# Attention of an iteration a quarter of its places later, where the second expert stream runs alone, and without the filler transposes

## What is computed

```python
x = x + 0.5 * _L0_ffn_ref(_layernorm(x), router_w, w1, w2)      # stream f1
x = x + _L0_attn_ref(_layernorm(x), W_qkv, W_out)               # stream at
x = x + 0.5 * _L0_ffn_ref(_layernorm(x), router_w, w1, w2)      # stream f2

# experts: 8 of them, widths 4 x 128 and 4 x 256; each token takes the best two
probs = sigmoid(xf @ router_w.T); topw, sel = top_k(probs, 2); topw /= topw.sum() + 1e-20
y = sum over the chosen e of topw_e * (relu(xf @ W1[e]) ** 2) @ W2[e]

# attention: 16 heads of 8, no softmax
q_feat = elu(rope(q) * SCALE) + 1;  k_feat = elu(rope(k)) + 1
kv = einsum('bhtd,bhtv->bhdv', k_feat, v);  k_sum = k_feat.sum(axis=2)
out = einsum('bhtd,bhdv->bhtv', q_feat, kv) / max(einsum('bhtd,bhd->bht', q_feat, k_sum), 1e-6)
x = x + out.reshape(B, T, D) @ W_out
```

## Time and profile before

| | us |
|---|---|
| median of 3 runs | 780.99 (779.64 to 781.48) |
| the profiled execution, its own time | 781.09 |
| its span, first to last instruction | 779.3 |
| mean granted TensorE clock | 0.991 of full |

### The profile page before, as it was taken

The page is one execution under the profiler, slowest core; times in us unless marked ns, Lnnn a source line. Parts: engine busy times, 40 slices in busy tenths (PEclk is TensorE's granted clock), DMA queues, the critical chain, the costliest instruction groups (busy, mean ns, idle before and its releaser), DMA issues.

```text
span 779.3 us, 13297 instructions
## 1 busy us (share of the span) xinstructions
PE 728.0 (93%) x3736; PEld 595.7 (76%) x3736; DVE 583.5 (75%) x1832; ACT 597.2 (77%) x1220; POOL 686.9 (88%) x664
## 2 busy tenths in 40 slices
PE   6799898789999999999999999999999998989887
PEld 6676676678888888888888888888887877767765
DVE  4767887877778786978788787978686777676543
ACT  4688768577888888798888888797879675766765
POOL 3899887769999999999999999999999868666886
PEclk9999999999999999999999999999999999999999
DMA  5553312312233333312233333313123303303330
GB/s 183 190 191 109 109 24 87 109 47 79 95 110 123 109 124 109 120 64 87 87 108 123 109 124 110 120 45 127 66 109 122 124 2 108 123 1 123 122 123 27
DMA packets 31160, 79.38 MB, mean 102 GB/s; under 512 B 3312, under 2 KB 14448, under 8 KB 31088
## 3 DMA queue, kind: packets, MB, share of 16 engines
q1 hardware_dynamic: 30800, 78.47, 29.7%
q10 hardware_dynamic: 288, 0.07, 0.1%
HBM read 73.81 MB, written 4.72 MB: 101 GB/s over the span
## 4 chain that ended last, share of the span: by engine, by line
POOL 26%; PE 26%; DVE 23%; issue 11%; ACT 8%; DMA 3%; DVEq 1%; POOLq 0%; ACTq 0%; SPq 0%
POOL h_lo L906 16%; DVE hid L1093 6%; POOL root_f L900 4%; PE bank L517 3%; PE bank L519 3%; PE bank L537 3%; PE bank L518 3%; PE bank L539 3%; PE bank L538 3%; ACT h_hi L763 2%; DMA g_all_f<-rows_f 2%; POOL x_lo_at L894 2%; DVE pick_f L1071 2%; PE bank L498 2%; PE bank L613 2%
## 5 line engine op out<-in xcount | busy, mean ns | idle before, releaser
L906 POOL TENSOR_TENSOR h_lo<-hid,h_hi 128x512 fp32r<-128x512 f32 x384 | 494.0, 1313 | 59.0 <-ACT h_hi L763 58.6
L1093 DVE SCALAR_TENSOR_TENSOR hid<-bank,g_all_f 128x512 f32<-128x512 f32 x384 | 263.3, 686 | 133.0 <-PE bank L519 93.9
L752 ACT ACTIVATE hid<-hid 128x512 f32<-128x512 f32 x384 | 229.2, 624 | 40.1 <-DVE hid L1093 40.0
L763 ACT ACTIVATE h_hi<-hid 128x512 fp32r<-128x512 f32 x384 | 226.4, 623 | 4.9 <-ACT hid L752 0.8
L517 PE MATMUL bank<-x_hi_f,w_hi 128*128 128x512 f32 x384 | 164.3, 428 | 13.7 <-DVE hid L1093 13.5
L537 PE MATMUL bank<-h_hi,w_hi 128*128 128x512 f32 x384 | 154.4, 402 | 7.1 <-POOL h_lo L906 6.9
L539 PE MATMUL bank<-h_hi,w_lo 128*128 128x512 f32 x384 | 152.6, 397 | 0.0
L519 PE MATMUL bank<-x_hi_f,w_lo 128*128 128x512 f32 x384 | 152.4, 397 | 0.0
L518 PE MATMUL bank<-x_lo_f,w_hi 128*128 128x512 f32 x384 | 152.1, 396 | 0.0
L538 PE MATMUL bank<-h_lo,w_hi 128*128 128x512 f32 x384 | 151.9, 396 | 0.0
L517 PEld LDWEIGHTS bank<-x_hi_f,w_hi 128*128 128x128 f32 x384 | 73.2, 191 | 37.0 <-DVE hid L1093 21.5
(11 more groups left out here) (112 smaller groups left out, 1053.7 us busy)
## 6 DMA issues: line engine op xcount, KB each, us to landing
g_all_f<-rows_f SPq DMA_DIRECT2D x128, 512.0 KB, 5.5
x_sb<-in_x SPq DMA_DIRECT2D x16, 256.0 KB, 3.0
out_x<-x_sb SPq DMA_DIRECT2D x16, 256.0 KB, 7.1
g_all_f<-in_w SPq DMA_DIRECT2D x2, 768.0 KB, 6.5
con<-in_const SPq DMA_DIRECT2D x1, 584.0 KB, 6.0
rows_f<-g_row_f SPq DMA_DIRECT2D x32, 16.0 KB, 1.4
g_all_f<-in_wqkv SPq DMA_DIRECT2D x1, 192.0 KB, 6.4
con<-in_const ACTq DMA_DIRECT2D x1, 68.0 KB, 3.0
```

The source lines that it names most:

```text
L752: fn(h, h, ACT.Square).then_inc(s_sq[s], 1)
L763: fn(h_hi[:, c, :], hid[:, c % STAGE, :], ACT.Copy).then_inc(s_hhi[s], 1)
L906: gp.tensor_tensor(h_lo[:, c, :], hid[:, c % STAGE, :], h_hi[:, c, :].bitcast(F32), ALU.subtract).then_inc(s_hlo[s], 1)
L1093: v.scalar_tensor_tensor(hid[:, c % STAGE, :], hp[c % 2][:], 0.0, g_all[s][:, EXPERT[c], :], ALU.max, ALU.mult).then_inc(s_z[s], 1)
```

## The change

In the iterations where f2 runs alone (t = 15, 16, 17) every part of attention from state to projection stands later: on TensorE state, attend, attn_transpose and out_proj each by a quarter (three jobs), on VectorE the mask by a place and the three steps of normalisation together behind weighted(10), on ScalarE the copy of the transposed attention behind the squares of quarter 4. add_attention stays where it was. The 16 filler transposes ahead of state are gone, 48 in all. Other iterations are not touched.

```diff
             def state(n):
                 pe.wait_ge(A["v"], value(n * BG + BG))
-                if alone("f2", n + 1):
-                    keep_busy(a1, 16)
                 pe.wait_ge(A["kf"], value(n + 1))
...
     TensorE, iteration(t, par)
                 quarter(t, 0, par)
-                state(t - 2)
+                if not alone("f2", t - 1):
+                    state(t - 2)
                 logits("f1", t + 2)
...
                 quarter(t, 1, par)
+                if alone("f2", t - 1):
+                    state(t - 2)
                 weight_rows("f2", t + 1 - SHIFT, t, 1)
-                attend(t - 2)
+                if not alone("f2", t - 1):
+                    attend(t - 2)
                 quarter(t, 2, par)
+                if alone("f2", t - 1):
+                    attend(t - 2)
                 transpose("at", t - 1, t, 2)
                 quarter(t, 3, par)
-                attn_transpose(t - 2)
+                if not alone("f2", t - 1):
+                    attn_transpose(t - 2)
...
                 quarter(t, 4, par)
-                out_proj(t - 2)
+                if alone("f2", t - 1):
+                    attn_transpose(t - 2)
+                else:
+                    out_proj(t - 2)
                 q(t - 1)
                 logits("f2", t + 2 - SHIFT)
                 quarter(t, 5, par)
+                if alone("f2", t - 1):
+                    out_proj(t - 2)
...
     ScalarE, iteration(t, par)
                 squares(t, 3)
-                copy_attnT(t - 2)
+                if not alone("f2", t - 1):
+                    copy_attnT(t - 2)
                 evacuate_x("f2", t + 2 - SHIFT, t, 2)
...
                 exp_logits("f2", t + 2 - SHIFT)
                 squares(t, 4)
+                if alone("f2", t - 1):
+                    copy_attnT(t - 2)
                 squares(t, 5)
...
     VectorE, iteration(t, par)
-                mask_state(t - 2)
+                if not alone("f2", t - 1):
+                    mask_state(t - 2)
                 weighted(t, 5)
                 best_two("f1", n1)
+                if alone("f2", t - 1):
+                    mask_state(t - 2)
                 weighted(t, 6)
...
                 weighted(t, 10)
+                if alone("f2", t - 1):
+                    normalise(t - 2, 0)
+                    normalise(t - 2, 1)
+                    normalise(t - 2, 2)
                 high_part("at", t - 1, 0)
```

More of the change, by code:

```diff
@@ L1227, in iteration @@
                 weighted(t, 7)
-                normalise(t - 2, 0)
+                if not alone("f2", t - 1):
+                    normalise(t - 2, 0)
                 weigh_two("f1", n1, 0)
                 weighted(t, 8)
-                normalise(t - 2, 1)
+                if not alone("f2", t - 1):
+                    normalise(t - 2, 1)
                 weigh_two("f1", n1, 1)
                 weighted(t, 9)
-                normalise(t - 2, 2)
+                if not alone("f2", t - 1):
+                    normalise(t - 2, 2)
                 weighted(t, 10)
+                if alone("f2", t - 1):
+                    normalise(t - 2, 0)
+                    normalise(t - 2, 1)
+                    normalise(t - 2, 2)
                 high_part("at", t - 1, 0)
```

## The result

The changed kernel takes 783.85 us (median of 16 runs, 782.02 to 787.4), the kernel before 780.17 us (778.25 to 782.32, 16 runs): ratio 1.0048, 95% interval 1.0036 to 1.006. That is 3.7 us slower. The forecast was 785.4, range 781.5 to 787.5, slower.

What follows compares the result with a forecast made beforehand. No engine is full in t = 15 to 17, so order and waits set the length, through VectorE's add_attention. Waits for the copy +2.3 and clock falls +2.1 give +4.4 us on 780.99: 785.4, range 781.5 to 787.5.

Steps and rivals of the forecast that it cites:

- order part: From q_features to add_attention: waits for the copied attention cost +0.3, +1.1, +0.9 us in t = 15, 16, 17, sum +2.3.
- clock part: In t = 15 to 17: clock falls behind new TensorE idle cost 3.15 us if all three occur; 2.1 taken.
- Fillers cost nothing on the path and cover the clock: Ahead of state: the 16 transposes lie beside TensorE's 1.35 us wait; removal saves 0 us, but they cover the clock.
- The mask is not later: VectorE's mask in t = 16: at about 668.05 against 668.20 before, though state is 1.9 us later.
- its wait on weighted(0): TensorE in t = 16: up(4) needs the bank weighted(0) empties at 664.70 to 665.38; a mask over 1 us later contradicts this.
- The logits' gain: Router logits in t = 16: done at 678.9, so exp at 678.95 against 680.10, a gain of 1.15 us.
- The projection waits for ScalarE's copy: TensorE's projection, t = 15 to 17: waits 1.4 to 1.8 us for the transposed attention's copy, now behind squares and copies.
- VectorE's unbroken half behind it passes all of this on.: From add_attention to the next q_features: VectorE works without a pause, so the whole +2.3 us delay passes on.
- Two falls of three were taken: Three new idle gaps of 3.1 us: two clock falls assumed, 2.1 us, each low stretch some 3.4 us.
- a fall begins only behind its wait: TensorE's clock: a fall starts after the idle wait ends (724, wait ended 723.20), a reason to take two of three.
- With the clock held: Rival 1: the clock holds through the new idle, only the copied-attention waits remain, +2.3 us, 783.3; chance 0.27.
- rival 2: ScalarE's copy is in time and projection goes right behind down(17): t = 15 to 17 sum -1.3 us, 779.8; chance 0.12.

## Why the prediction was right, and where it was not

- **Sign and size.** +3.7 us measured, +4.4 forecast, from an order part (2.3) and a clock part (2.1). The runs give 0.9 and 2.8. One part was too large by 1.4 and the other too small by 0.7, so that the total came within 0.7 us is partly luck.
- **Fillers cost nothing on the path and cover the clock.** Right: taking them out alone cost 2.7 us, and from q to a the loss lies in the two iterations in which the clock fell.
- **The mask is not later.** Right where the clock holds: with the fillers back it starts 3.93 us behind q_features in t = 16, forecast 3.95, before 4.10. In the changed kernel it starts 6.01 us behind, over 1 us later, which the prediction took for a sign that its wait on weighted(0) is wrong. It was not that, but the low clock. The iterations of the changed kernel, 33.8 and 30.5 us, also lie outside the forecast 31 to 33.
- **The logits' gain.** Direction right, size not: with the fillers back, exp starts 15.30 us behind q_features against 16.00 before, a gain of 0.70 in place of 1.15. The step that was off is x_hi_at behind the three steps of normalisation: 11.54 us behind q_features against 10.57 before, 1.0 later and not 0.5: weighted(10), which stands ahead of them, ended 10.05 us behind q_features and not 9.6.
- **The projection waits for ScalarE's copy.** Right in each iteration, 1.13 to 1.15 us where I had 1.4 to 1.8. What follows from it, q to a with the fillers back: forecast +0.3, +1.1, +0.9; measured -0.03, +1.59, +1.10, with the caveat above on the first.
- **"VectorE's unbroken half behind it passes all of this on."** This is the step that failed. It read "works without a pause" as "fixed in length". (The half that the prediction gives as 683.63 to 664.10 runs from 653.39 to 664.10, and the next from 683.63 to 694.32.) In that half cw_f was 0.5 us too long in t = 15 and 16, and 1.0 in t = 17, held by GpSimd; a later add_attention finds GpSimd's operation over and gets this back. With the 0.8 of the tail, the order part was therefore 0.9, not 2.3.
- **The clock.** The idle was right (3.1 forecast; 3.10, 3.24, 3.22). Two falls of three were taken, three came in the profiled execution, and the one in t = 16 lasted 7 us, not 3.4. Against the run with fillers back the falls cost 1.27, 2.47 and 0.62 us from q to a, forecast 0.65, 1.6 and 0.9. Not every execution had all of them: of the 16 runs the six with the lowest mean clock (0.984 and 0.985) took 785.3 to 787.4 us, the six with the highest (0.989 to 0.993) 782.0 to 783.2, and one low stretch of 3.4 us is 0.002 of that mean. The run at 0.993 has lost 5.5 us of clock in all, 1.8 of it by estimate in the first 40 us as in the profiled execution; the rest is room for two stretches of 1.7 and not for three. Where the falls of the other runs lay, the mean clock of a whole execution doesn't say. Even the second six are 1.8 us and more over before, so how much of the loss is the clock's stays known only within the intervals above. One reason for taking two of three, that a fall begins only behind its wait, is wrong: in t = 16 and 17 it began inside it.
- **Rivals.** With the clock held (fillers back) the kernel was at 780.4, not 783.3: the mechanism was right, the price too high by what cw_f gave back. With the copy in time and the clock held, the q to a and a to q terms sum to -1.25, the -1.3 of rival 2, though by other terms (t = 16 by 0.17 slower, the halves behind faster), so that agreement is luck; with the tail it was 2.5 us under before.

## What to carry to other kernels

A part that is moved later along the list of one engine is late on every other, and the one to check is the copy between two engines: give it the idle stretch that its engine has, not the like-named place. Filler work beside a wait is not free to remove: it cost nothing on the path here, and without it the clock took 2.7 us. Whether real work in its place holds the clock as well, no run shows. And where a row of a small operation is several times as long as its twins, look which other engine's operation ends with it: one such row moved by one place was worth 4.0 us here by the ratio (3.3 by the medians), part of it perhaps through the clock in the tail; the whole rearrangement with its two faults mended, 2.5 (2.7).

## What the hardware showed that I had not expected

- A VectorE operation of 128 x 8 elements takes 0.15 to 0.17 us alone and up to 1.16 us beside a GpSimd subtraction of 128 x 512, ending within 0.03 us of it. Where it started first, at 653.18 against GpSimd's 653.22 in the kernel without fillers, it took 0.15. The profile counts this as VectorE's busy time, so neither waits nor idle time show it.
- The same TensorE idle is followed by a fall of the clock to 1.2 GHz in some executions and not in others: 2.67 to 2.69 us in the tail, with a fall in before and with the fillers back, none in the changed kernel; 1.84 us in the tail, with a fall where down(3) is first, none in the kernel before without fillers; 3.29 us in t = 15 without a fall and 3.40 us in t = 16 with one, in the same execution. A low stretch lasted from about 3.4 to about 7 us.
